# Inverse roots of the second sum's norms: from GpSimd's power to shift and Newton steps on VectorE

## The reference, cut to what matters

```python
def _layernorm(x, g, b):
    mu = jnp.mean(x, axis=-1, keepdims=True)
    var = jnp.mean((x - mu) ** 2, axis=-1, keepdims=True)
    return (x - mu) * jax.lax.rsqrt(var + LN_EPS) * g + b
...
x = _layernorm(x + out, ln1_g, ln1_b)
ff = jax.nn.relu(x @ W1 + b1) @ W2 + b2
x = _layernorm(x + ff, ln2_g, ln2_b)
```

## Time and profile before

| what | value |
|---|---|
| median of 3 runs | 10629.57 us (10617.3 to 10630.08) |
| the profiled execution, its own time | 10620.97 us |
| its span, first to last instruction | 10619.4 us |
| TensorE, matmuls busy | 7940.7 us, 75% |
| VectorE busy | 6394.1 us, 60% |
| GpSimd busy | 6257.5 us, 59% |
| ScalarE busy | 1702.6 us, 16% |
| mean granted TensorE clock | 0.817 |

### The profile page before, as it was taken

One profiled execution on the slowest core, in us unless ns is written; L12 is line 12 of the kernel. 1 busy time (PEld: TensorE's weight loads), 2 busy tenths in 40 slices (PEclk: granted clock), 3 DMA queues, 4 the chain that ended last, 5 costly groups with the idle time before them and its releaser, 6 DMA issues. The chain is left out here.

```text
span 10619.4 us, 140467 instructions
## 1 busy us (share of the span) xinstructions
PE 7940.7 (75%) x33573; PEld 5648.0 (53%) x33573; DVE 6394.1 (60%) x21684; ACT 1702.6 (16%) x3275; POOL 6257.5 (59%) x6431
## 2 busy tenths in 40 slices
PE   4644666666666888888888857887887887777779
PEld 3423455555555666666666645555555555444447
DVE  6865777777775555555555546666666666544432
ACT  0000000000002333333343311010010010011110
POOL 2224777777775787777777766666666666400002
PEclk7657888888887888888888868888888888777779
DMA  1015333333332111111111113333333333222225
GB/s 46 25 47 132 108 108 107 107 106 109 108 108 49 16 16 16 16 16 16 16 16 16 17 42 91 90 94 93 92 92 93 93 92 92 74 62 62 62 68 169
DMA packets 460523, 738.75 MB, mean 70 GB/s; under 512 B 141888, under 2 KB 313957, under 8 KB 459537
## 3 DMA queue, kind: packets, MB, share of 16 engines
q0 software_dynamic: 235408, 494.89, 18.2%
q1 hardware_dynamic: 211414, 224.43, 7.3%
q10 hardware_dynamic: 13240, 15.44, 0.5%
HBM read 624.06 MB, written 108.44 MB: 69 GB/s over the span
## 5 line engine op out<-in xcount | busy, mean ns | idle before, releaser
L897 POOL DMA_INDIRECT sum_gathered<-table,sum_idx x3600 | 3496.6, 971 | 1256.1 <-issue 1008.8
L962 PE MATMUL sum_agg_res<-sum_gathered,sum_lay 125*125 125x256 f32 x7200 | 2296.3, 458 | 1072.1 <-DVE all_sums L947 415.2
L1468 POOL DMA_INDIRECT sorted_recs<-fin_rec,fin_pos x1700 | 2115.5, 1244 | 502.8 <-issue 498.6
L962 PEld LDWEIGHTS sum_agg_res<-sum_gathered,sum_lay 125*125 125x125 f32 x7200 | 1483.1, 221 | 1714.4 <-DVE all_sums L947 1242.8
L947 DVE TENSOR_TENSOR all_sums<-all_sums,sum_agg_res 125x256 f32 x3600 | 1510.3, 420 | 1051.8 <-PE sum_agg_res L962 880.6
L928 DVE TENSOR_SCALAR sum_lay<-all_lane,sum_dloc_now,sum_w_now 125x125 f32<-125x125 f32 x3612 | 1294.8, 359 | 20.8 <-DVE sum_xn_tiles L1079 16.2
L1899 PE MATMUL fin_ps_up<-fin_tokens_T,fin_w 128*128 128x250 f32 x3200 | 990.6, 446 | 0.0
L1907 PE MATMUL fin_ps_dn<-fin_w,fin_hidden 128*125 128x256 f32 x3200 | 855.9, 402 | 10.4 <-DVE fin_acc L1537 10.4
L1899 PEld LDWEIGHTS fin_ps_up<-fin_tokens_T,fin_w 128*128 128x128 f32 x3200 | 692.0, 230 | 165.8 <-issue 65.6
L1537 DVE SCALAR_TENSOR_TENSOR fin_acc<-fin_ps_dn,fin_comb,fin_acc 125x256 f32<-125x256 f32 x800 | 383.2, 482 | 567.0 <-PE fin_ps_dn L1907 555.1
L1907 PEld LDWEIGHTS fin_ps_dn<-fin_w,fin_hidden 128*125 128x125 f32 x3200 | 598.5, 196 | 127.2 <-issue 49.4
(11 more groups left out here) (481 smaller groups left out, 11411.5 us busy)
## 6 DMA issues: line engine op xcount, KB each, us to landing
sum_gathered<-table,sum_idx POOLq DMA_INDIRECT x3600
sorted_recs<-fin_rec,fin_pos POOLq DMA_INDIRECT x1700
slice_weights<-slices_sw SPq DMA_DIRECT2D x50, 500.0 KB
out_sw<-slice_weights SPq DMA_DIRECT2D x50, 480.0 KB
deg_x_tiles<-in_x SPq DMA_DIRECT2D x100, 125.0 KB
sum_x_tiles<-in_x SPq DMA_DIRECT2D x100, 125.0 KB
fin_x<-in_x SPq DMA_DIRECT2D x100, 125.0 KB
x<-fin_acc SPq DMA_DIRECT2D x100, 125.0 KB
```

Source lines behind the costliest of these rows:

```text
L897: eng.indirect_dma_start(out=self.rows[:, s % self.RING, :], out_offset=None, in_=self.table, in_offset=bass.IndirectOffsetOnAxis(ap=self. ...
L962: eng.matmul(self.res[s % self.RES][:, 0, :], self.lay[:, g % 2, l, :], self.rows[0:P, s % self.RING, :], start=True, stop=True).then_inc( ...
L1468: eng.indirect_dma_start(out=k.sorted_recs, out_offset=bass.IndirectOffsetOnAxis(ap=pos[:, n, r:r + 1], axis=0), in_=rec[:, n, r, :], in_o ...
```

## The change

The inverse roots are no longer worked out on GpSimd, whose stream in this stage is now a plain loop of gathers. VectorE works them out itself, in twelve instructions on 125x4 values, each of which waits for the one before: add the epsilon, shift the bits right by one, subtract from a constant to have a first guess, and then three Newton steps of three instructions. The chain for the second norm of the supertile before stands behind the sums of half-group 1, that for the first norm behind those of half-group 10; the last one follows the loop.

```diff
-        neg_half = sb("neg_half", [P, TS])
...
         ve = sb("var_eps", [P, 2, TS])
+        root = sb("root_now", [P, 2, TS])
         rs = sb("rstds", [P, 2, TS])
...
+        ROOT_SEED = 1597463007.0
...
         @block.gpsimd
         def _(eng):
-            eng.memset(neg_half[:], -0.5).then_inc(S.power_ready, 1)
-            eng.wait_ge(S.power_ready, 1)
-
-            def rstd(which, i):
-
-                eng.wait_ge(mv_ready[which], i + 1)
-                eng.nop(nofuse=True)
-                eng.tensor_scalar(ve[:, which, :], mv[:, which, :, 1], LN_EPS, None, ALU.add).then_inc(rs_steps[which], 1)
-                eng.wait_ge(rs_steps[which], i + 1)
-                eng.nop(nofuse=True)
-                eng.tensor_tensor(rs[:, which, :], ve[:, which, :], neg_half[:], ALU.pow).then_inc(rs_ready[which], 1)
-
-            def run(i):
-                first = isinstance(i, int)
-                for half in range(2):
-                    agg.take_indices(i, half)
-                    for g in range(half * GRPS // 2, (half + 1) * GRPS // 2):
-                        if g == 3 and not first:
-                            rstd(1, i - 1)
-                        if g == 7:
-                            rstd(0, i)
-                        agg.gather_group(i, half, g)
-
-            supertiles(eng, run)
-            rstd(1, k.NSUP - 1)
+            with eng.Fori(0, k.NSUP) as i:
+                agg.gather_half(i, 0)
+                agg.gather_half(i, 1)
...
+            def rstd(which, i):
+
+                v, y, r = ve[:, which, :], root[:, which, :], rs[:, which, :]
+                ready = rs_steps[which]
+                eng.wait_ge(mv_ready[which], i + 1)
+                eng.nop(nofuse=True)
+                eng.tensor_scalar(v, mv[:, which, :, 1], LN_EPS, None, ALU.add).then_inc(ready, 1)
+                eng.wait_ge(ready, i * 11 + 1)
+                eng.tensor_scalar(y.bitcast(I32), v.bitcast(I32), 1, None, ALU.logical_shift_right).then_inc(ready, 1)
+                eng.wait_ge(ready, i * 11 + 2)
+                eng.tensor_scalar(r.bitcast(I32), y.bitcast(I32), -1.0, ROOT_SEED, ALU.mult, ALU.add)\
+                   .then_inc(ready, 1)
+                for turn in range(3):
+                    eng.wait_ge(ready, i * 11 + 3 + turn * 3)
+                    eng.scalar_tensor_tensor(out=y, in0=r, scalar=-0.5, in1=r, op0=ALU.mult, op1=ALU.mult)\
+                       .then_inc(ready, 1)
+                    eng.wait_ge(ready, i * 11 + 4 + turn * 3)
+                    eng.tensor_tensor(y, y, v, ALU.mult).then_inc(ready, 1)
+                    eng.wait_ge(ready, i * 11 + 5 + turn * 3)
+                    eng.scalar_tensor_tensor(out=r, in0=y, scalar=1.5, in1=r, op0=ALU.add, op1=ALU.mult)\
+                       .then_inc(rs_ready[which] if turn == 2 else ready, 1)
...
                 if n == 1:
-                    after(eng, rs_ready[0], i)
                     statistics(0, i)
...
                 if n == 1:
-                    after(eng, rs_ready[1], i)
                     statistics(1, i)
...
                         agg.add(i, h // 2, l)
+                    if h == 1 and not isinstance(i, int):
+                        rstd(1, i - 1)
...
                         add_attention(i, h - 8)
+                    elif h == 10:
+                        rstd(0, i)
...
             supertiles(eng, run)
+            rstd(1, k.NSUP - 1)
```

More of the change, by code:

```diff
@@ L2096, in sum_layer1 @@
         w_in, x_in, stored = (sem(n) for n in ("w_in", "x_in", "stored"))
-        names = ("consts", "power_ready", "T1_done", "T1_kept", "q_done", "q_below", "q_kept", "q_exp", "phi_ready",
+        names = ("consts", "T1_done", "T1_kept", "q_done", "q_below", "q_kept", "q_exp", "phi_ready",
                  "den_done", "z_chain", "phin_ready", "attn_done", "y_added", "y1_steps", "y1_ready", "T2_done",
@@ L2100, in sum_layer1 @@
         S = Shared()
-        (S.consts, S.power_ready, S.T1_done, S.T1_kept, S.q_done, S.q_below, S.q_kept, S.q_exp, S.phi_ready,
+        (S.consts, S.T1_done, S.T1_kept, S.q_done, S.q_below, S.q_kept, S.q_exp, S.phi_ready,
          S.den_done, S.z_chain, S.phin_ready, S.attn_done, S.y_added, S.y1_steps, S.y1_ready, S.T2_done, S.T2_kept,
```

## The result

The changed kernel takes 10716.15 us in the median (10713.8 to 10730.57, 4 runs), the kernel before 10626.51 us beside it (10617.3 to 10630.08, 4 runs): 90 us more, ratio 1.0089 with a 95% interval of 1.0071 to 1.0106. The profiled execution spans 10713.5 us at a granted clock of 0.811.

The account below looks back on a forecast made before the run. No engine was full; VectorE's unbroken run in half-group 10, with TensorE waiting behind it, was taken as the binding path. Chains gave 49 us, 54 with the clock: 10675, plus 8.6 to the median, 10684 us; range 10645 to 10740.

Parts of the forecast that it names:

- No wait for gathered blocks; GpSimd's stand is slack: Second sum: TensorE waits for no gathered block after 6900 us, so removing GpSimd's 282.8 us of waits buys nothing.
- Twelve links of 0.19 us, 2.2 us: Each chain of twelve dependent VectorE instructions, twice a supertile (block of four tiles), costs 11 x 0.19 + 0.12 = 2.2 us.
- The plan's chain: Six dependent links in the plan of layer 1, 0.19 us each, taken as nearest model for the new chains.
- The estimate of 0.8 us: A chain's cost from 58 cycles plus elements at 0.96 GHz, 65 ns an instruction; not used for the sum.
- Half-group 10, net 1.7 us: First normalisation's chain on VectorE: 2.2 us, less 0.3 of absorbed waits and 0.2 given back, per supertile.
- the 0.2 given back by the removed power: Half-group 10's first sum-up comes earlier without GpSimd's power beside it: 0.2 us taken of 0 to 0.4.
- Half-group 1, 0.2 us: Second normalisation's chain hides in VectorE's 3.06 us stand; the tile-number load behind it costs 0.2 of 0 to 0.4 us.
- The sum without the clock: Over the second sum, 25 x (1.7 + 0.2) = 48 us, and under 1 us at the end: 49 us.
- The clock: TensorE's clock levels between supertiles: cost 49 us if shares stay, 58 if all distances become long; 54 taken.
- Rival 1: TensorE drops to 1.2 GHz in every supertile on top of the chain: 105 us, 10735; chance 0.15.
- 119 and more as a sign against: Distances between supertiles in the changed profile of 119 us and more, or still 112.6, would show the forecast wrong.
- the forecast's own case: Chain on VectorE's path plus clock, 10684 us, supertiles 115.5 to 116.0 us apart, range 10655 to 10710; chance 0.65.

Follow-up runs that it names:

- e9: The changed kernel with GpSimd waiting for the first norm's means ahead of the gathers of group 7, computing nothing; third chip, 10750.26 us, 128 over before.
- e6: Against the kernel before, only the first norm's chain goes to VectorE, the second norm's power stays on GpSimd; second chip, 10685.47 us, ratio 1.0049.
- e8: The kernel before with GpSimd's power for the first norm ahead of the gathers of group 8 instead of 7; second chip, 10693.89 us, ratio 1.0058.
- e10: Against the kernel before, only the second norm's chain goes to VectorE, the first norm's power stays on GpSimd; third chip, 10683.96 us, ratio 1.0051.
- e11: The changed kernel with each chain moved between the load of tile numbers and the first sum-up of half-groups 2 and 10; 10721.89 us, ratio 1.0086.
- e7: The changed kernel with one Newton step in place of three; second chip, 10657.66 us, ratio 1.0024 against before.
- e12: The changed kernel with chains moved behind the tile-number loads of half-groups 2 and 10, two Newton steps for three; 10723.56 us, ratio 1.0091 against before.
- e4: The changed kernel with one Newton step in place of three; first chip, 11580.07 us, ratio 0.9823 against before.
- e5: The changed kernel timed once more, on the second chip; 10720.68 us, ratio 1.0083 against before.

## Why the prediction was right

The forecast was 10684 us with a range of 10645 to 10740; it came out 32 us higher, inside the range, and slower as forecast. Step by step:

1. **No wait for gathered blocks; GpSimd's stand is slack.** As forecast, its waits moved to TensorE's products. But this holds only for a chip like that of the trace. On the first chip of the experiments the stand binds, and e9 suggests that the freedom gives some 24 us back, by the clock, even where nobody waits for a gather. The prediction had costed that at nothing.
2. **Twelve links of 0.19 us, 2.2 us.** 0.20 and 2.26 us. The plan's chain was the right row. The estimate of 0.8 us from the Trainium skill, page "VectorE: DVE Perf Modes", section on the TRN2 errata, was not: each of these instructions takes 0.16 or 0.17 us here. The same section of the Trainium skill says of the 58 cycles that they come out too low for a single instruction, which the prediction doesn't pass on.
3. **Half-group 10, net 1.7 us.** 2.29: the 0.3 absorbed came (0.35), but the 0.2 given back by the removed power turned into 0.38 lost. This step failed in sign, and its reading failed with it. The prediction held GpSimd's power to be what makes the 1.59 us of half-group 10 longer than the 1.18 of half-group 6. The load's own records are 1.41 and 1.43 us there; in half-group 6 it merely starts 0.5 us ahead of the layout. It isn't the gathers either: e6, e8 and e10 have GpSimd at different work beside that load and keep 1.88 to 1.91 us, e9 has it held like before and shows 2.25. The runs in which the load starts late are those with two chains of twelve links in VectorE's loop, e11 among them; two chains of six or nine links (e7, e12) or one of twelve leave it early. What in a longer program does it is open.
4. **Half-group 1, 0.2 us.** 0.62, where at most 0.4 was foreseen: from layout to sum-up, read at 1.18 to 1.59 us, 1.75 pass in this place (e10). A term mis-sized within its own mechanism.
5. **The sum without the clock** was 49 us and is 25 x (2.29 + 0.62) = 73. TensorE's stands, some 83 us longer, agree with it but for 10 us that no row explains. These 24 us are most of the 36 by which the price was short (54 foreseen, 90 measured).
6. **The clock** was the term with the least ground. It assumed that the levels go on in their shares, or that all short distances become long ones. e8 shows the second case by itself, 62 us. In the change the levels are new ones (115.2, 117.5, 119.0), and 90 - 73 = 17 us are left; TensorE's busy time gives the clock some 10 of them, where the forecast had 5. Rival 1, the step on top of the chain, gave 105 us. The measured time lies between it and the forecast, but not by its mechanism: a step of 3.35 us in each of 17 short distances would have made TensorE's busy time some 57 us longer, as it did in e8.

Distances were forecast near 115.5 to 116.0, with 119 and more as a sign against. They are 114.2 to 119.3, mean 117.27: by that test the forecast's own case was half wrong. Its own range ended at 10710, and the result lies 6 us above; the wider range holds it because it reached to rival 1. So the mechanism was right in the main, a chain on VectorE's path that costs its length, and that the time fell inside the range is in part luck.

No run beats the kernel before on the second and third chip. On the first, one Newton step on VectorE does by 211 us; three steps without the hold would by an estimate (e4 less the 63 us between e5 and e7) gain some 150.

## What to carry to other kernels

Read from a dependent chain nearby what a link costs, and ask where the receiving engine has no idle time: twelve tiny instructions on an engine that is 63% busy cost nearly their whole length in half-group 10 (2.26 us less 0.35), while the power they replace had been waiting for others anyway. In a loop whose distance between turns comes in two or more values, look at the values before pricing a delay: an edit that delays nothing seen by more than about 0.1 us moved all turns but the first to the longer one here, so a few us of change in each turn can't be read as path time without a run that moves nothing but the timing. The busy time of the same matmuls in both traces tells a cost in clock from a cost in stands. And time a kernel on more than one chip before calling an engine's wait slack.

## What the runs showed of the hardware

- A load of six register values on VectorE's queue takes 1.41 to 1.43 us in half-groups 6 and 10 (0.81 us in 8 and 12) and held what stands behind it: in e11 1.17 us of idle time stayed ahead of instructions that don't use the registers.
- The granted clock repeats within a supertile: e8 has the 0.78 and 0.88 of before's long distances behind its aggregate at 7459.74, and its supertiles stand 116.0 to 116.1 us apart, 23 times in a row (from aggregate to aggregate).
- The first sum-up of half-group 10 stands 1.88 or 2.25 us behind the aggregate, by kernel, with at most 0.03 us of scatter over 19 supertiles.
- A normalisation part of four instructions (L2205) takes 1.38 us in every supertile of before and 1.49 in every one of e8, where only GpSimd's order differs.
- The same 6716 matmuls keep TensorE busy for 2087 us in before and for 2143 us in e8, at a mean granted clock of 0.84 and 0.82. The changed kernel has 2097 us at the same 0.82, so the mean alone doesn't tell what the clock costs.
- The same program takes 10622 to 10632 us in all other comparisons and 11791 on the first chip of the experiments, and the rate of the gathers in the first sum goes with it, 107 against 82 GB/s.
